# Building edge matrices with row-tiled 64x128 products instead of 128x128 products

## What is computed

```
x = LN(x + L0(x)); x = LN(x + L1(x)); x = LN(x + L2(x)); x = LN(x + L3(x))
L0: h = x + segment_sum(x[src], dst);  relu(h W1 + b1) W2 + b2 + x Wres + bres
L1: two rounds of h + mean over edges of h[src], each followed by two dense products
L2: four steps xc + 0.1 tanh(xc A' + neigh + bias), neigh weighted by edge_weight and degrees
L3: relu(segment_sum((x W + b)[src] + (edge_attr We + be), dst))
```

## Time and profile before

| | us |
|---|---|
| median of 3 runs (lowest, highest) | 1265.88 (1265.79, 1266.02) |
| the profiled execution, its own time | 1267.85 |
| span in its profile (first to last instruction) | 1266.1 |
| PE, PEld, DVE, ACT busy in the span | 1097.1, 668.7, 611.9, 289.5 |
| mean granted clock of PE | 0.957 |

### The profile page before, as it was taken

The page is one execution under the profiler, slowest core; times in us unless marked ns, Lnnn a source line. Parts: engine busy times, 40 slices in busy tenths (PEclk is TensorE's granted clock), DMA queues, the critical chain, the costliest instruction groups (busy, mean ns, idle before and its releaser), DMA issues.

```text
span 1266.1 us, 19105 instructions
## 1 busy us (share of the span) xinstructions
PE 1097.1 (87%) x7527; PEld 668.7 (53%) x7527; DVE 611.9 (48%) x1063; ACT 289.5 (23%) x610; POOL 104.4 (8%) x92
## 2 busy tenths in 40 slices
PE   5014677877887999999999999999999999999998
PEld 5014676766776445444554654456454555455555
DVE  1857999999958332453232223223123223434222
ACT  2014777767753010110000000000000001112100
POOL 4883000000000000000000000001000000000000
PEclk9556999999999999999999999999999999999999
DMA  5421375575568656657776698749986598754920
GB/s 162 128 61 40 154 304 227 227 303 215 240 291 369 253 185 272 253 203 280 279 273 262 237 379 335 285 190 350 380 306 265 185 382 348 298 208 181 424 80 26
DMA packets 39237, 311.54 MB, mean 246 GB/s; under 512 B 10873, under 2 KB 13161, under 8 KB 17298
## 3 DMA queue, kind: packets, MB, share of 16 engines
q1 hardware_dynamic: 27983, 298.70, 60.1%
q0 software_dynamic: 11200, 12.09, 3.4%
HBM read 245.45 MB, written 65.24 MB: 245 GB/s over the span
## 4 chain that ended last, share of the span: by engine, by line
PE 67%; DVE 14%; issue 11%; POOL 5%; ACT 1%; DVEq 1%; DMA 1%; POOLq 0%
PE ps L1135 41%; PE ps L1125 14%; DVE arena L635 5%; PE ps L1083 5%; DVE arena L628 4%; POOL arena L430 3%; POOL arena L438 2%; PE ps L1047 2%; PE ps L1095 1%; PE ps L1043 1%; PE ps L994 1%; DVE arena L707 1%; DVE arena L709 1%; DVE arena L710 1%; DVE stats L643 1%
## 5 line engine op out<-in xcount | busy, mean ns | idle before, releaser
L1135 PE MATMUL ps<-arena 125*128 125x500 f32 (+1 forms) x700 | 269.5, 540 | 0.0
L1135 PE MATMUL ps<-arena,parts_even 125*128 125x500 f32 (+1 forms) x700 | 267.8, 538 | 0.0
L1238 PE MATMUL ps<-arena 128*128 128x100 f16 x1625 | 144.6, 207 | 62.6 <-DVE arena L635 59.5
L1135 PEld LDWEIGHTS ps<-arena 125*128 125x128 f32 x700 | 123.7, 190 | 128.3 <-issue 128.3
L1135 PEld LDWEIGHTS ps<-arena,parts_even 125*128 125x128 f32 x700 | 123.0, 189 | 127.3 <-issue 127.3
L1238 PEld LDWEIGHTS ps<-arena 128*128 128x128 f16 x1625 | 126.4, 99 | 77.4 <-ACT arena L916 61.8
L1125 PE MATMUL ps<-arena 125*128 125x500 f16 (+2 forms) x700 | 142.7, 358 | 2.7 <-issue 2.5
L1240 PE MATMUL ps<-arena 128*128 128x50 f16 x1625 | 140.4, 188 | 0.0
L1240 PEld LDWEIGHTS ps<-arena 128*128 128x128 f16 x1625 | 123.8, 97 | 1.3
L914 ACT ACTIVATE arena<-ps 128x400 f16<-128x400 f32 x208 | 104.9, 504 | 73.7 <-PE ps L1240 68.4
L896 ACT ACTIVATE XT<-ps 128x500 f32<-128x500 f32 (+1 forms) x49 | 26.5, 540 | 397.1 <-PE ps L1095 397.0
(11 more groups left out here) (171 smaller groups left out, 928.5 us busy)
## 6 DMA issues: line engine op xcount, KB each, us to landing
arena<-weight_mats SPq DMA_DIRECT2D x24, 3250.0 KB, 11.4
arena<-weight_mats SPq DMA_DIRECT2D x24, 3000.0 KB, 11.1
arena<-count_mats SPq DMA_DIRECT2D x18, 3125.0 KB, 11.7
weight_mats<-arena SPq DMA_DIRECT2D x13, 3125.0 KB, 13.0
count_mats<-arena SPq DMA_DIRECT2D x13, 1562.5 KB, 5.4
arena<-weight_mats SPq DMA_DIRECT2D x4, 1625.0 KB, 6.5
arena<-weight_mats SPq DMA_DIRECT2D x4, 1500.0 KB, 6.3
arena<-count_mats SPq DMA_DIRECT2D x3, 1562.5 KB, 6.3
```

The costliest lines, as they stand in the source:

```text
L1135: ins = t.matmul(o, xs[:, k, :], rhs, start=(k == 0), stop=(k == NC - 1))
L1238: t.matmul(ps[:, bank, o:o + 2 * LO], hot_hi[b][:, T, :], hot_lo[b][:, T, 0:2 * LO], start=(e == 0), stop=False, skip_group_check=True)
```

## The change

The lo one-hot becomes LO = 26 columns wide (one spare column, so that it stays even): the code is lo - 1 for both nodes. Each tile is multiplied in four matmuls on 64 partitions each: the count and high part (52 columns) of node 0 and of node 1, then the low part (26 columns) of each. Node j goes to bank + j. Units become 15 of 9, 8 and 8 tiles, steps 34, 33, 33 and 25 tiles. The `sum_counts` blocks stand ahead of the products of units 1 to 14 instead of behind units 1 to 15, the first of them with the wait for `counts_out`. Columns of a pair are now stored as (j, t).

```diff
-LO = 2 * NC
-STEP_AT = (0, 32, 64, 96, NP)
+LO = NC + 1
+UNITS = 15
+UNIT_AT = tuple(25 * (u // 3) + (0, 9, 17)[u % 3] for u in range(UNITS)) + (NP,)
+UNITS_TO = (4, 8, 12, UNITS)
+STEP_AT = tuple(UNIT_AT[u] for u in (0,) + UNITS_TO)
...
-            v.memset(code_base[0:64], -2.0)
-            v.memset(code_base[64:128], -1.0)
+            v.memset(code_base, -1.0)
...
-                    if n == GCOL:
-                        pa = pa.rearrange("p (a t j) -> p a j t", a=2, j=2)
-                        t1 = t1.rearrange("p (a j t) -> p a j t", a=2, j=2)
-                        xt = xt.rearrange("p (a j t) -> p a j t", a=2, j=2)
...
-                    ins = s.activation(lo_c[...], src, ACT.Identity, bias=code_base, scale=2.0)
+                    ins = s.activation(lo_c[...], src, ACT.Identity, bias=code_base, scale=1.0)
...
+                    bank, n = 2 * (u % SLOTS3), UNIT_AT[u + 1] - UNIT_AT[u]
+                    src = ps[:, bank:bank + 2, 0:2 * LO * n].rearrange("p b (t m) -> p m b t", m=2 * LO)
+                    return src[:, LO * weight:LO * weight + NC]
...
-                                rhs = slot[:, 0:1, ks, 0:2 * NP:2].rearrange("p q a n -> p (q a n)")
+                                rhs = slot[:, 0:1, ks, 0:NP].rearrange("p q a n -> p (q a n)")
...
                 def pair(q, odd, first=False):
                     for u in range(UNITS):
+                        if not first:
+                            if u == 1:
+                                pe.wait_ge(counts_out, UNITS * q)
+                            if u:
+                                a, z = ((u - 1 + d) * NC // (UNITS - 1) for d in (0, 1))
+                                sum_counts(q - 1, 1 - odd, range(a, z))
+                        if UNIT_AT[u] == STEP_AT[step]:
                             pe.wait_ge(hots_ok, STEPS * q + step + 1)
+                        pe.wait_ge(weights_out, UNITS * q + u - SLOTS3 + 1 + OUT_PAD)
+                        bank = 2 * (u % SLOTS3)
+                        for T in range(UNIT_AT[u], UNIT_AT[u + 1]):
+                            o, e = 2 * LO * (T - UNIT_AT[u]), T - STEP_AT[step]
+                            for a, z in ((0, 2), (2, 3)):
+                                for j in range(2):
+                                    rows = slice(SLOTS * j, SLOTS * j + SLOTS)
+                                    ins = t.matmul(ps[:, bank + j, o + (LO if a else 0):o + 2 * LO], hot_hi[b][rows, e, :],
+                                                   hot_lo[b][rows, e, LO * a:LO * z],
+                                                   start=(T == UNIT_AT[u] and not a), stop=False, skip_group_check=True)
                         ins.then_inc(sums_ok, 1)
```

More of the change, by code:

```diff
@@ L42 @@
 FE = 8
-LO = 2 * NC
-STEP_AT = (0, 32, 64, 96, NP)
-STEPS = len(STEP_AT) - 1
[L46 to L53, removed]
+LO = NC + 1
+UNITS = 15
+SLOTS3 = 3
+UNIT_AT = tuple(25 * (u // 3) + (0, 9, 17)[u % 3] for u in range(UNITS)) + (NP,)
+UNITS_TO = (4, 8, 12, UNITS)
+STEP_AT = tuple(UNIT_AT[u] for u in (0,) + UNITS_TO)
+STEPS = len(STEP_AT) - 1
 SUM_BANK = 7
@@ L185, in build_program @@
         STEP_MAX = max(z - a for a, z in zip(STEP_AT, STEP_AT[1:]))
-        hot_hi = [at(75000 + 17792 * i, 128, [STEP_MAX, 128], F16) for i in range(2)]
-        hot_lo = [at(83192 + 17792 * i, 128, [STEP_MAX, 3 * LO], F16) for i in range(2)]
+        hot_hi = [at(75000 + 14008 * i, 128, [STEP_MAX, 128], F16) for i in range(2)]
+        hot_lo = [at(83704 + 14008 * i, 128, [STEP_MAX, 3 * LO], F16) for i in range(2)]
         iota_hi = at(114000, 128, [128], F16)
@@ L704, in first_sum @@
                     if not general:
-                        if n == GCOL:
-                            inv = inv.rearrange("p (a j t) -> p a j t", a=2, j=2)
                         link(v.tensor_tensor(t1, pa, xt, ALU.subtract))
@@ L873, in _ @@
                 if k == 1:
-                    ins = s.activation(lo_c[:, 4 * g:4 * g + n, :, :], src, ACT.Identity, bias=code_base, scale=2.0)
+                    ins = s.activation(lo_c[:, 4 * g:4 * g + n, :, :], src, ACT.Identity, bias=code_base, scale=1.0)
                 else:
@@ L900, in sums_of @@
                 def sums_of(u, weight):
[L902 to L907, removed]
+                    bank, n = 2 * (u % SLOTS3), UNIT_AT[u + 1] - UNIT_AT[u]
+                    src = ps[:, bank:bank + 2, 0:2 * LO * n].rearrange("p b (t m) -> p m b t", m=2 * LO)
+                    return src[:, LO * weight:LO * weight + NC]
                 def leave(q, odd, u):
-                    n = 2 * (LAST_T if u == UNITS - 1 else UT)
-                    cols = slice(2 * UT * u, 2 * UT * u + n)
+                    cols = slice(UNIT_AT[u], UNIT_AT[u + 1])
                     act.wait_ge(sums_ok, UNITS * q + u + 1 + SUMS_PAD)
-                    s.activation(stg_c[odd][:, :, cols].rearrange("p k (t j) -> p k t j", j=2), sums_of(u, 0),
+                    s.activation(stg_c[odd].rearrange("p k (j t) -> p k j t", j=2)[:, :, :, cols], sums_of(u, 0),
                                  ACT.Copy).then_inc(counts_out, 1)
-                    s.activation(stg_w[odd][:, :, cols].rearrange("p k (t j) -> p k t j", j=2), sums_of(u, 1),
+                    s.activation(stg_w[odd].rearrange("p k (j t) -> p k j t", j=2)[:, :, :, cols], sums_of(u, 1),
                                  ACT.Copy).then_inc(weights_out, 1)
@@ L921, in sum_out @@
                     act.wait_ge(agg0_done, q + 3)
-                    s.activation(sum0[:, bass.ds(q * (2 * NP), 2 * NP)].rearrange("p (j t) -> p j t", j=2),
-                                 ps[:, SUM_BANK, 0:2 * NP].rearrange("p (t j) -> p j t", j=2), ACT.Copy,
+                    s.activation(sum0[:, bass.ds(q * (2 * NP), 2 * NP)], ps[:, SUM_BANK, 0:2 * NP], ACT.Copy,
                                  scale=1.0 / X_SCALE).then_inc(sum0_out, 1)
@@ L1133, in weight_steps @@
                         else:
-                            rhs = slot[:, 0, k - W_KS[m][0], 0:2 * NP:2]
+                            rhs = slot[:, 0, k - W_KS[m][0], 0:NP]
                         ins = t.matmul(o, xs[:, k, :], rhs, start=(k == 0), stop=(k == NC - 1))
@@ L1219, in sum_counts @@
                             ins.then_inc(agg0_done, 1)
[L1221 to L1225, removed]
                 def pair(q, odd, first=False):
                     for u in range(UNITS):
-                        step = sum(UT * u >= a for a in STEP_AT) - 1
+                        step = sum(UNIT_AT[u] >= a for a in STEP_AT) - 1
@@ L1230, in pair @@
                         b = step % 2
-                        if UT * u == STEP_AT[step]:
-                            pe.wait_ge(hots_ok, STEPS * q + step + 1)
[L1233 to L1242, removed]
@@ L1243, in pair @@
-                        ins.then_inc(sums_ok, 1)
[L1244 to L1248, removed]
+                        if not first:
[4 more added lines that the diff above has]
+                                sum_counts(q - 1, 1 - odd, range(a, z))
```

## The result

| | us |
|---|---|
| before, median of 4 runs | 1265.95 (1265.79 to 1268.61) |
| changed kernel, median of 4 runs | 1345.53 (1342.39 to 1349.56) |
| ratio, 95% interval | 1.0625, 1.0589 to 1.0661 |
| span and own time of its profiled execution | 1347.8 and 1349.56 |

A forecast was written before the change was run, and what follows sets the result against it. DVE bounds the build at 19.2 us a pair; after the change PE takes over at 7.5 + 5.4 + 2.8 + 0.8 = 16.5 us. Over twelve pairs the build ends 36.5 us earlier: 1229 us, range 1203 to 1310.

The forecast's parts named there:

- PE after the change, term by term: Step summing PE's work and waiting in the build: 16.5 us a pair, more than DVE's 14.56, so PE becomes the bound.
- round 0's products: PE, build: 50 matmuls a pair at 0.107 us each, 5.4 us a pair, unchanged.
- edge products: PE, build: four narrow matmuls a tile, the two array halves overlapping; 7.5 us a pair, ends 7.0 and 14.25.
- switches: PE, build: 28 changes a pair between 125-row and 64-row products, 0.10 us each, 2.8 us a pair.
- the new wait: PE, build: `sum_counts` for chunk 0, now behind unit 0, waits for ACT's last copies and `sum_out`; 0.8 us a pair.
- DVE's term: DVE, build: fewer one-hot elements cut its work from 19.2 to 14.56 us a pair, so it gives up 4.6 us.
- serial rival: PE, build: array halves take turns, edge products cost 14.25 us and a pair 22.7; slower, 1304 us; chance 0.27.
- PE without waits for DVE in the middle of the build: Sign expected in the profile after: mid-build, PE no longer waits for DVE, whose 14.6 us a pair leaves idle time.
- A wait of PE for ACT at each pair's unit 1: Sign expected in the profile after, from the wait costed at 0.8 us a pair.
- ACT's copies: ACT, build: PSUM copies plus `sum_out` stay at 12.4 us a pair, new 52-column stride costed at nothing; not the next bound.
- The rounds: After the build: the natural column order removes strided views of `first_sum`; costed at nothing, at most 1 us either way.
- The sum: PE's pair in the build: 7.5 + 5.4 + 2.8 + 0.8 = 16.5 us.

The follow-up runs named there:

- short-loop kernel: The changed kernel with one pair instead of two in PE's loop, 1147 instructions, same matmuls: 1237.74 us, 0.9794 of the kernel before.
- one-block: The short-loop kernel with round 0's products of a pair in one block ahead of unit 1 instead of fourteen blocks: 1283.37 us, 1.0137 of the kernel before.
- seven-block: The short-loop kernel with round 0's products in seven blocks, ahead of every second unit, instead of fourteen: 1244.95 us, 0.9836 of the kernel before.
- kernel with the blocks behind: The short-loop kernel with round 0's fourteen blocks behind units 1 to 14, the wait for `counts_out` there too: 1228.38 us, 0.9696 of the kernel before.
- unrolled kernel: The changed kernel with PE's loop written out, all 13 pairs in a row without a branch: 1306.71 us, 1.0321 of the kernel before.

## Why the prediction was wrong

**What failed** is the step "PE after the change, term by term": its four terms (round 0's products, edge products, switches, the new wait) were taken for the whole of PE's pair, and the 500 instructions more a pair had no term. With the stream of instructions taken care of, the same edit gives 1237.7 us and not 1345.5, 9 us above the forecast. The 108 us are stalls for instructions and their consequence, a granted clock of 0.77 instead of 0.99 in 160 to 320 us. None of the rivals named it either. The page of before held the hint: 38 blocks on q8, and in the trace none of them between 174 and 380 us, though PE went through its loop six times; that had to be read as "the loop fits", and then "will 2242 fit" was the question.

**DVE's term was right.** 14.56 us a pair forecast; in the short-loop kernel DVE is busy 147.56 us of 160, and a pair is 15.91: 147.56 / 160 x 15.91 = 14.7 us of work, the rest waits for PE. DVE did cease to be the bound, but PE did not take over alone: each waits about 1 us a pair for the other.

**The edge products** were forecast at 7.5 us with ends of 7.0 and 14.25: 125 x 0.052 = 6.5 us, a little under the lower end, since the slot with 52 and 26 columns is 26 ns and not 28. The serial rival falls. Of the two pages of the Trainium skill, "TensorE: Matmul & The Clock Gate" (Part 3) had it right, with its start 4 ns apart: in the trace of the short-loop kernel the two of a couple start 3 to 4 ns apart. The caution in "TensorEngine Tiling (Array Packing)" (Instruction Overhead) did not hold here. Four weight loads a tile did not matter.

**The switches** were forecast at 0.10 us from the f32 rows; about 0.09 by the trace, 28 x 0.09 = 2.5 us a pair. But their price could not be had back by fewer blocks: the one-block and seven-block kernels were slower, by waits for ACT and DVE and a lower clock.

**The new wait,** 0.8 us a pair for ACT, is not there. In the short-loop kernel round 0's first products of a pair follow unit 0 after 0.56 us (236.73 to 237.29), as they follow every unit of 9 tiles, and from 160 to 320 us PE never waits for ACT's sum. PE stands still before unit 0 instead, 1.15 us for DVE, and when unit 0 is through, at 237.29 us, ACT has ended its sum (236.47 + 0.38 us). So of the signs named, "PE without waits for DVE in the middle of the build" and "A wait of PE for ACT at each pair's unit 1" both failed.

**ACT's copies,** forecast at 12.4 us a pair with their new stride at nothing, were not quite free. A counts copy of 400 elements takes 578 ns by the median in the short-loop kernel, before 507. In the one-block kernel, where PE waits for ACT, the copies of four units in a row start 0.85 us apart (248.49 to 251.88 us): 15 x 0.85 + 0.4 = 13.1 us a pair, of 15.91.

**The rounds.** The natural column order was costed at nothing: from PE's first dense product to the end it is 890.9 us before, 889.9 with the short loop, 895.5 in the changed kernel. The kernel with the blocks behind, which has the same order, has 892.9, so the order is free within some 3 us; the 5 us of the changed kernel as it stands stay unexplained.

**The sum.** Forecast were 15.7 us of PE's work and 0.8 of waiting, 16.5. Measured are 14.8 of work and 1.15 of waiting for DVE, 15.9. The wait is the beat of two buffers: DVE's first step of a pair waits 0.97 us for PE to free one (rows above), and PE, whose last step has 25 tiles only, then waits for that step of 34.

## What to carry to other kernels

When an edit multiplies the instructions of a loop, count them: an engine that ran a loop without fetches may refetch it in every pass, and the limit is sharp (here between 1444 and 1644 instructions a pass on PE). Past it the kernel before lost 1.3 to 1.8% where PE had time to spare, the changed kernel, where it had none, 9% against its version with the short loop. The instruction queue's blocks in the page of before, and whether they pause during the loop, tell whether it fits now; "issue" waits in the middle of a burst, worst while large stores run, tell that it no longer does. Two row-tiled halves of the array do pay for narrow products, if neighbours in program order alternate between the halves.

## What the runs showed of the hardware

- Four products of 64x52 and 64x26 with four weight loads take 52 ns at full clock when the halves alternate; a stop at a late block lasts up to 5.8 us on PE while stores run (463 to 465 GB/s in the stop shown), and up to 4.5 us with them out of the way.
- Straight code is not safe either: the unrolled kernel, 1100 instructions in 16 us, lost 69 us to the short loop.
- PE can be busy 157.6 of 160 us and be granted 1.2 GHz all the while, when consecutive products stay in one half of 64 rows; 32 of them then take 1.12 us, alternating ones at the same clock 0.67.
